# Self-attention probabilities: split in row layout and transposed by DMA, in a three-stage decoder layer pipeline

## The reference, cut to what matters

```
scaled = h / norm(h);  q = scaled Wq' + bq;  v = scaled Wv' + bv
probs = softmax(q (q A)' / 16)                 # 2048 x 2048, one head
x = x + (probs v) * norm(h)                    # self-attention
x = x + softmax(q k' / 8) v Wo                 # cross-attention, 1601 keys, 4 heads of 64
x = x + FFN of the one expert that argmax of the gate picks   # 4 experts, 256 -> 1024 -> 256, gelu
```

## Time and profile before

| | |
|---|---|
| median of 3 runs | 842.32 us (841.49 to 844.99) |
| the profiled execution | its span, first to last instruction, is 848.8 us; no other time of it is given |
| PE busy | 755.1 us, 89% |
| DVE busy | 653.2 us, 77% |
| ACT busy | 457.9 us, 54% |
| POOL busy | 138.9 us, 16% |
| mean granted clock of TensorE | 0.954 of full speed |
| tile steps in the profile | about 95 to 695 us; expert blocks about 707 to 849 us |

### The profile page before, as it was taken

How to read it: one execution, slowest core, us unless ns; L and a number is a source line. 1 busy time by engine, 2 the same in 40 slices (tenths; PEclk the granted TensorE clock), 3 DMA queues, 4 the chain that set the end, 5 groups by cost and what they waited for, 6 DMA issues and landing times. The chain is left out here.

```text
span 848.8 us, 19493 instructions
## 1 busy us (share of the span) xinstructions
PE 755.1 (89%) x6136; PEld 681.1 (80%) x6137; DVE 653.2 (77%) x1619; ACT 457.9 (54%) x922; POOL 138.9 (16%) x246
## 2 busy tenths in 40 slices
PE   3988799999999999999999999999986416999996
PEld 2778689989889899898898998988975314999995
DVE  5984647788888888888888888888878465777773
ACT  2544626566566665666666656666665432334332
POOL 3100110120211201202112012021120410222221
PEclk9999989999999999999999999999978856999999
DMA  6242110010101000000010000000123260111110
GB/s 211 70 138 70 47 29 7 24 29 15 29 12 28 28 6 28 24 16 28 12 28 28 6 28 24 17 28 12 54 113 99 101 235 26 36 39 39 37 33 15
DMA packets 25525, 39.32 MB, mean 46 GB/s; under 512 B 3086, under 2 KB 18704, under 8 KB 25360
## 3 DMA queue, kind: packets, MB, share of 16 engines
q1 hardware_dynamic: 23232, 33.02, 12.5%
q0 software_dynamic: 2256, 5.83, 2.0%
HBM read 28.82 MB, written 10.41 MB: 46 GB/s over the span
## 5 line engine op out<-in xcount | busy, mean ns | idle before, releaser
L1076 ACT ACTIVATE ps_cross<-flip 128x512 f16<-128x512 f32 (+1 forms) x256 | 125.0, 514 | 116.5 <-PE flip L795 91.0
L1318 DVE TENSOR_TENSOR ps_cross<-flip,ps_cross 128x512 f16<-128x512 f32 (+1 forms) x256 | 145.0, 583 | 24.8 <-ACT ps_cross L1076 20.4
L795 PE MATMUL flip<-ident,exp_cross 128*128 128x128 f32 (+1 forms) x832 | 131.8, 282 | 9.9 <-DVE ps_cross L1318 6.5
L1277 ACT ACTIVATE exp_cross<-exp_cross,xneg 128x1024 f32<-128x1024 f32 (+1 forms) x128 | 122.7, 960 | 19.2 <-DVE xneg L1492 19.1
L784 PE MATMUL scores<-keys_cross,qt 128*128 128x402 f32 x512 | 127.6, 372 | 5.3 <-DVE xneg L1492 3.5
L795 PEld LDWEIGHTS flip<-ident,exp_cross 128*128 128x128 f32 (+1 forms) x832 | 95.8, 143 | 18.1 <-DVE ps_cross L1318 8.3
L672 PE MATMUL scores<-keys_self,u_tile 128*128 128x512 f32 x384 | 102.2, 403 | 6.4 <-issue 4.9
L806 PE MATMUL cross_out<-vals_cross,ps_cross 128*128 128x128 f16 (+1 forms) x832 | 102.5, 224 | 5.5 <-issue 4.9
L771 PE MATMUL flip<-vals_self,ps_self 128*128 128x256 f32 x768 | 103.8, 289 | 0.0
L806 PEld LDWEIGHTS cross_out<-vals_cross,ps_cross 128*128 128x128 f16 (+1 forms) x832 | 76.4, 101 | 28.3 <-issue 20.4
L771 PEld LDWEIGHTS flip<-vals_self,ps_self 128*128 128x128 f32 x768 | 96.7, 194 | 0.0
(11 more groups left out here) (207 smaller groups left out, 1189.2 us busy)
## 6 DMA issues: line engine op xcount, KB each, us to landing
w_stage<-W SPq DMA_DIRECT2D x8, 1024.0 KB, 5.4
u_dram<-u_out SPq DMA_DIRECT2D x4, 1024.0 KB, 5.9
u_tile<-u_dram SPq DMA_DIRECT2D x16, 256.0 KB, 2.7
mask_tile<-mask SPq DMA_DIRECT2D x16, 200.1 KB, 2.4
rows<-rows_dram SPq DMA_DIRECT2D x19, 130.0 KB, 2.1
x_all<-x SPq DMA_DIRECT2D x4, 512.0 KB, 5.8
x_tile<-x SPq DMA_DIRECT2D x16, 128.0 KB, 2.0
b_row<-b SPq DMA_DIRECT2D x1, 2048.0 KB, 8.9
```

Source lines behind the costliest of these rows:

```text
L795: tr = pe.transpose(flip[0:rows, bank(use), n * P:(n + 1) * P], exp_cross[:, h % 2, m * P:m * P + rows], ident[:, :])
L1076: return act.activation(out, in_, ACT.Copy, **kw)
L1277: act.activation(exp_cross[:, h % 2, cols], exp_cross[:, h % 2, cols], ACT.Exp, bias=xneg[:, h % 2, 1:2], scale=-1.0, accum_out=xden[:, ha ...
L1318: return dve.tensor_tensor(out, full, hi, ALU.subtract)
```

## The change

`self_flip` and ps_self go. ACT and DVE now split exp_self as it lies, 128 tokens by 1024 keys at a time, into two float16 parts (self_p), and SP transposes each part by `dma_start_transpose` into self_pt, four transfers a tile. `self_values` takes halves of 8 blocks and waits for the two transfers of its half. vals_self becomes float16, scaled by a bound on the values that is made in the prologue (a reduction of the weights, an all-reduce over partitions and four small steps), and norms are scaled back. The exponentials of the self scores get a constant factor by way of sneg. The cross transposes alternate between banks 0 and 1 of flip, and all small uses and self_out have bank 2, so cross transpose n waits for the low part of group n-2. The body orders of PE, ACT and DVE change with that: both halves of self values stand behind cross values (0, 1), x1 and its statistics move behind the low part of cross group (1, 0), and the gate moves behind cross scores (3, 0). A tensor `apart` of 16 KB per partition is only reserved.

The diff, cut to its core. Of PE's body the new order stands alone, without the removed lines; the old order is in the functions above. In the bodies, every flip bank of a small use becomes SMALL.

```diff
@@ -42,6 +44,8 @@
 BLOCKS = T + E - 1
 XROWS = SPARE + E * P
 V_TOP = 4096.0
+SELF_V_TOP = 32768.0
+SELF_P_TOP = 16384.0
 XHALF = 2 * 512
...
-BANKS = {("x", 2, 2): 0, ("x", 2, 3): 1, ("xn",): 2, ("x", 3, 0): 0, ("xq",): 2, ("qs",): 2,
-         ("x", 3, 1): 1, ("x", 3, 2): 2, ("s", 0): 0, ("x", 3, 3): 1, ("s", 1): 2, ("s", 2): 0,
-         ("sum",): 2, ("s", 3): 0, ("o",): 1, ("x", 0, 0): 0, ("wo",): 1, ("x", 0, 1): 1,
-         ("x", 0, 2): 0, ("x", 0, 3): 2, ("x", 1, 0): 1, ("x", 1, 1): 0, ("x3",): 2, ("x", 1, 2): 1,
-         ("gate",): 2, ("x", 1, 3): 0, ("x", 2, 0): 1, ("x", 2, 1): 2, ("rank",): 0}
...
+def cross_bank(h, g):
+    return (NG * h + g) % 2
+
+
+SMALL = 2
+
+
+def group_of(j, h, g):
+
+    return 16 * (j - (2 if h == 3 or h == 2 and g >= 2 else 1)) + NG * h + g
 
...
-    vals_self = sb("vals_self", [P, T, 2, D], F32R, keep)
+    vals_self = sb("vals_self", [P, T, 2, D], F16, keep)
+    apart = sb("apart", [P, T * D], F32, keep)
 
...
-    ps_self = sb("ps_self", [P, 4, 2, 512], F32R, loop)
+    self_p = sb("self_p", [P, 2, N], F16, loop)
+    self_pt = sb("self_pt", [P, 2, T, P], F16, loop)
     mask_tile = sb("mask_tile", [P, M], U8, loop)
...
@@ -475,6 +480,19 @@
             if k < T - 1:
                 sp.wait_ge(scores_ready, 4 * j + 4)
                 loads_a(j + 1)
+            if k < T:
+                for half in range(2):
+                    at = slice(half * N // 2, (half + 1) * N // 2)
+                    to = slice(half * T // 2, (half + 1) * T // 2)
+                    sp.wait_ge(self_p_hi, 2 * j + half + 1)
+                    if k >= 1:
+                        sp.wait_ge(self_p_used, 2 * j)
+                    sp.dma_start_transpose(out=self_pt[:, 0, to, :], in_=self_p[:, 0, at]).wait_op(
+                        constants_set, CONSTANTS, "sem-ge").then_inc(self_turned[half], 16)
+                    sp.wait_ge(self_p_lo, 2 * j + half + 1)
+                    sp.dma_start_transpose(out=self_pt[:, 1, to, :], in_=self_p[:, 1, at]).wait_op(
+                        constants_set, CONSTANTS, "sem-ge").then_inc(self_turned[half], 16)
+            if k < T - 1:
                 sp.wait_ge(x1_ready, j + 1)
...
-        def self_flip(j, k, g):
-            use = ("s", g)
-            if g % 2 == 0:
-                pe.wait_ge(self_exp, 2 * j + g // 2 + 1)
-            for n in range(4):
-                m = 4 * g + n
-                tr = pe.transpose(flip[:, bank(use), n * P:(n + 1) * P], exp_self[:, m * P:(m + 1) * P], ident[:, :])
-            tr.then_inc(self_flipped, 1)
-
-        def self_values(j, k, g):
-            pe.wait_ge(self_p_lo, 4 * j + g + 1)
-            for n in range(4):
-                m = 4 * g + n
+        def self_values(j, k, half):
+            pe.wait_ge(self_turned[half], 32 * j + 32)
+            for m in range(half * T // 2, (half + 1) * T // 2):
                 for a, b in ((0, 0), (0, 1), (1, 0)):
-                    mm = pe.matmul(self_out[:, 0:D], ps_self[:, g, a, n * P:(n + 1) * P], vals_self[:, m, b, :],
+                    mm = pe.matmul(self_out[:, 0:D], self_pt[:, a, m, :], vals_self[:, m, b, :],
                                    start=(m == 0 and a == 0 and b == 0), stop=(m == T - 1 and a == 1))
             mm.then_inc(self_p_used, 1)
 
@@ -786,21 +798,23 @@
             mm.then_inc(cross_scores_ready, 1)
 
         def cross_flip(j, k, h, g):
-            use = ("x", h, g)
-            t = j - stage_of(use)
+            n = group_of(j, h, g)
             if g % 2 == 0:
-                pe.wait_ge(cross_exp_ready, 8 * t + 2 * h + g // 2 + 1)
+                pe.wait_ge(cross_exp_ready, n // 2 + 1)
+            if not (k == 1 and h == 0 and g < 2):
+
+                pe.wait_ge(cross_p_lo, n - 1)
             for n, m in enumerate(XG[g]):
                 rows = P if m < MC - 1 else MLAST
-                tr = pe.transpose(flip[0:rows, bank(use), n * P:(n + 1) * P], exp_cross[:, h % 2, m * P:m * P + rows], ident[:, :])
+                tr = pe.transpose(flip[0:rows, cross_bank(h, g), n * P:(n + 1) * P], exp_cross[:, h % 2, m * P:m * P + rows], ident[:, :])
             tr.then_inc(cross_flipped, 1)
...
-            t = j - (2 if (h, g) in ((2, 0), (2, 1)) else stage_of(("x", h, g)))
-            pe.wait_ge(cross_p_lo, 16 * t + 4 * h + g + 1)
+            at = group_of(j, h, g) + (0 if h != 2 or g >= 2 else -16)
+            pe.wait_ge(cross_p_lo, at + 1)
             if h == 0 and g == 0 and k >= 2:
-                pe.wait_ge(o_summed, t)
+                pe.wait_ge(o_summed, j - 1)
...
             if a:
                 self_scores(j, k, 0)
             if c:
+                cross_flip(j, k, 2, 2)
+            if a:
+                self_scores(j, k, 1)
+            if c:
+                cross_flip(j, k, 2, 3)
+            if b:
+                if k > 2:
                     pe.wait_ge(rank_used, j - 2)
+                small(xn_ready, j, xn_flipped, flip_row(xn))
             if a:
                 self_scores(j, k, 2)
             if c:
                 cross_flip(j, k, 3, 0)
             if b:
+                small(xt_lo, j, q_ready,
                       lambda out: three(out[:, 0:D], lambda a, c: xt[:, a, c, :], lambda b, c: wq_cross[:, b, c, :]))
             if a:
                 self_scores(j, k, 3)
             if c:
                 cross_values(j, k, 2, 0)
                 cross_values(j, k, 2, 1)
+            if b:
+                small(qs_lo, j, q_flipped, flip_queries)
+            if c:
+                cross_flip(j, k, 3, 1)
                 cross_values(j, k, 2, 2)
+                cross_flip(j, k, 3, 2)
                 cross_values(j, k, 2, 3)
+                cross_values(j, k, 3, 0)
+            if b:
+                cross_scores(j, k, 0, 0)
+            if c:
+                cross_flip(j, k, 3, 3)
+                cross_values(j, k, 3, 1)
+            if b:
+                cross_scores(j, k, 0, 1)
+            if c:
+                cross_values(j, k, 3, 2)
+            if b:
+                cross_scores(j, k, 1, 0)
+            if c:
+                cross_values(j, k, 3, 3)
+            if b:
+                cross_flip(j, k, 0, 0)
+                cross_scores(j, k, 1, 1)
+            if c:
 
                 if k == T + 1:
+                    pe.wait_ge(rank_used, j - 2)
+                small(o_ready, j - 1, o_flipped, flip_row(o_tile[:, :, :].rearrange("p h d -> p (h d)")))
+            if b:
+                cross_flip(j, k, 0, 1)
+                cross_values(j, k, 0, 0)
+            if c:
+                small(ot_lo, j - 1, wo_ready,
+                      lambda out: three(out[:, 0:D], lambda a, c: ot[:, a, c, :], lambda b, c: wo_cross[:, b, c, :]))
+            if b:
+                cross_flip(j, k, 0, 2)
+                cross_values(j, k, 0, 1)
+            if a:
+
+                if c:
+                    pe.wait_ge(x2_ready, j - 1)
+                elif b:
                     pe.wait_ge(qt_ready, j)
                 self_values(j, k, 0)
+            if b:
                 cross_flip(j, k, 0, 3)
                 cross_scores(j, k, 2, 0)
+                cross_values(j, k, 0, 2)
                 cross_flip(j, k, 1, 0)
+            if a:
+                self_values(j, k, 1)
+            if b:
+                cross_values(j, k, 0, 3)
                 cross_flip(j, k, 1, 1)
                 cross_scores(j, k, 2, 1)
+                cross_values(j, k, 1, 0)
                 cross_flip(j, k, 1, 2)
+                cross_values(j, k, 1, 1)
+            if c:
+
+                if a:
+                    pe.wait_ge(x1_ready, j + 1)
+                small(xn3_ready, j - 1, x3_flipped, flip_row(xn3))
+            if b:
                 cross_scores(j, k, 3, 0)
                 cross_flip(j, k, 1, 3)
+            if c:
+                small(x3t_ready, j - 1, gate_ready, gate)
+            if b:
+                cross_values(j, k, 1, 2)
                 cross_flip(j, k, 2, 0)
                 cross_scores(j, k, 3, 1)
+                cross_values(j, k, 1, 3)
                 cross_flip(j, k, 2, 1)
+            if c:
+                pe.wait_ge(logits_ready, j - 1)
...
+            at = slice(half * N // 2, (half + 1) * N // 2)
+            act.wait_ge(self_exp, 2 * j + half + 1)
             if k >= 1:
-                act.wait_ge(self_p_used, 4 * j + g - 3)
-            copy(ps_self[:, g, 0, :], flip[:, bank(("s", g)), :]).then_inc(self_p_hi, 1)
+                act.wait_ge(self_turned[half], 32 * j)
+            copy(self_p[:, 0, at], exp_self[:, at]).then_inc(self_p_hi, 1)
 
         def body(j, k):
             a, b, c = k < T, 1 <= k <= T, k >= 2
...
             if c:
                 cross_hi(j, k, 3, 3)
             if k == T:
                 weights_hi(1)
             if k == T + 1:
                 weights_hi(4)
-            if a:
-                self_hi(j, k, 1)
-                self_hi(j, k, 2)
             if b:
                 cross_exp(j, k, 0, 0)
-            if a:
```

(56 more changed lines are left out.)

219 lines of the change are left out of this document (68 added, 151 removed).

## The result

The changed kernel takes 1033.4 us (1031.4 to 1036.5), the kernel before in the same session 843.7 us (841.5 to 846.2): 1.226 times as long, 95% interval 1.222 to 1.229. The forecast was 1000 us, slower, range 885 to 1055. Its profiled execution spans 1034.7 us, 185.9 more than the 848.8 before.

The account below looks back on a forecast made before the run. TensorE was taken to bound the loop before, with VectorE close behind. From the profiled 848.8 us, 120 for longer passes, 24 for the clock and 13 for edges gave 1006, less 6.5: 1000 us, range 885 to 1055.

Parts of the forecast that it names:

- (1): TensorE in the loop: sixteen transposes of exp_self go, saving 1.5 us a pass.
- (2): Self values on TensorE: 48 matmuls with 2-byte operands take 0.12 us instead of 0.127, saving 0.3 us a pass.
- gap 1: TensorE idle 3.3 us before the first cross transposes, awaiting the first cross exponential; a pass grows by 3.2 us.
- (3) to (6): Queue walk of one pass: three TensorE gaps and late waits make 42.5 us, 8.6 more; 120 us over 14 passes.
- (6): Late in the pass, the gate moved behind cross scores (3,0) adds net waits of 0.3 us.
- Gaps 2 and 3: TensorE idle before cross values (0,0) and (0,1), awaiting low parts from VectorE: 2.05 and 3.05 us.
- (7): Clock falls to 1.2 GHz after the idle stretch, slowing self values: 1.7 us a pass, 24 us; bounds 0 and 5.5.
- (8): Four DMA transposes of 256 KB a tile on SP, 2.7 us each to landing, hidden at no cost.
- (9): Edges: prologue 2 us (bounds 0 to 3), k = 0 3, k = 1 5, k = T 3; together 13 us.
- A: Rival: TensorE stays the bound of the loop and has 1.8 us less a pass; 817 us, chance 6%.
- B: Rival: only the first TensorE gap is real, later hand-overs overlap better; 887 us, chance 8%.
- C: Rival: DMA transposes are slow, 8.9 us each, delaying the second half of self values; 1220 us, chance 9%.

Follow-up runs that it names:

- e_gap1: Changed kernel with the maximum and exponential of the first cross head moved ahead of the second half of the self split: 974.6 us, ratio 1.155.
- e_warm: Changed kernel, same order, with 48, 24 and 40 spare matmuls put into the three TensorE idle gaps of each full pass: 977.9 us, ratio 1.159.
- e_spread: Changed kernel with the prologue's GpSimd all-reduce replaced by VectorE and TensorE steps, nothing else: 1026.1 us, ratio 1.215.
- e_f16_spread: Kernel before with 2-byte self probabilities and values, the GpSimd all-reduce replaced by VectorE and TensorE steps: 836.7 us, ratio 0.990.
- e_twice: Changed kernel with every DMA transpose issued twice, the second into an unread tensor, self values waiting for both: 1040.0 us, ratio 1.231.
- e_dma_old_order: Kernel before, its three banks and order kept, with the row split, DMA transposes and 2-byte values: 879.6 us, ratio 1.042.
- e_f16_before: Kernel before, its order and TensorE transposes kept, with only self probabilities and values made 2-byte and scaled: 844.8 us, ratio 1.000.

## Why the prediction was right, and where it was off

The sign, the main mechanism and its size held. By its steps:

(1), (2) PE's savings. The 16 transposes are gone. The 2-byte matmuls go faster than I took: 24 of them from 400.01 to the next instruction at 402.63 in e_gap1, 0.109 us each, just beyond my lower bound (0.11; I took 0.12). In the kernel before's order that came to 0.5 us a pass. After the change the transposes' part falls into gap 1; the self values stand behind the gaps, so theirs shortens the pass.

(3) to (6) The walk through the queues was right: at the full clock each station is met within 0.3 us, and the pass of 42.3 within 0.2 of 42.5. The last agreement is in part luck, two misses that cancel: SV is 0.5 us shorter than taken, and the late waits of (6), taken as 0.3, are 0.50 and 0.25 us in e_warm. Gap 1 was put at 3.3 and is 3.28. One agreement has another cause than mine. I put the second self exponential at t = 11.6, 0.4 later than before, because CF(3,2) waits for a bank; it is at 404.88 - 393.26 = 11.6, but the first one, 2.04 us ahead of it, is already at 402.84, t = 9.6, before 9.1 (358.61 less the 349.49 of the earlier trace rows), right behind the copy of qt. The maximum behind sneg, which I called equal within 0.1 us, takes 0.34 and 0.08 us in its new form, before 0.16; that copy hides it. The copies took 1.05 to 1.08 us and the subtractions 1.21 to 1.23 (I took 1.0 and 1.15). Gaps 2 and 3 look smaller in the changed kernel (1.17 and 2.30 against 2.05 and 3.05) because PE's work between them is slower at 1.2 GHz: CV(0,0) stands at t = 23.8 instead of 22.4.

(7) The clock is the term that was mis-sized. I took 1.7 us a pass from two edge stretches, bounds 0 to 5.5; e_warm shows 4.1, that is 57 us instead of 24, and this is most of what lies between forecast and result. The edge stretches of the earlier trace rows were a bad measure of length: what counts is how much work stands in the low stretch, and here all between gap 1 and the end of SV's first half does, 15 us of it.

(8) The transposes: 2.7 us to landing, as taken, hidden in the loop. No wait names one of SP's other loads of the loop. But where nothing covers the transposes, in k = 0, PE waits 8.7 us for them. (9) The edges: k = 0 cost 2.2 (3 taken), k = 1 5.1 (5 taken). The prologue cost 10.3, taken as 2 with a bound of 3: I counted the all-reduce as a step of VectorE's chain and not as what POOL's next instruction stands behind. e_spread and e_f16_spread show 7.4 and 8.0 us of that to be the collective. k = T cost 1.5 (3 taken). The forecast sum was 157 us over the profiled execution before; the clock adds 33, the prologue 8; k = T takes 1.5 away, the long last step of that profiled execution 7, the walk at 42.3 instead of 42.5 another 3, k = 0 one: 186 but for rounding, as in the trace.

The rivals. A fell (passes of 46.4 us, PE busy 78%), B too (all three gaps are there), C by e_twice. The rule beside C, the Trainium skill's page "VectorE: DVE Perf Modes", section "The three transpose paths", gives 1309 ns for one block, a figure that doesn't carry over to this shape: a 128x1024 transpose of 2-byte elements, eight blocks, lands in 2.7 us and holds SP for 1.24, where eight times that figure, as an estimate, would be 10.5. The same page's section "Rules for kernel authors" advises TensorE for a 128x128 transpose whose result may go to PSUM. The times here agree: e_dma_old_order, with transposes by DMA, takes 879.6 us and e_f16_before, with transposes on TensorE, 844.8. In the loop most of the difference is waits for low parts, 29.9 us in twelve passes, and little of it the DMA's, 2.6.

## What to carry to other kernels

When work leaves the engine that bounds a kernel, ask which waits that work was covering: here 4.5 us of transposes and self values stood over the chain to the first cross exponential, and some 2 us saved a pass became 12.4 lost. Price an idle gap on TensorE with the dense work that stands behind it at the lower clock, and if such a gap can't be removed, cheap matmuls in it may pay. Price a small collective on GpSimd by what is queued behind it, and try it on VectorE and TensorE first.
